# Eight-core retention block: the decay scales broadcast by TensorE instead of by DMA

## The chip, the cores and the metric

The kernel runs on the 8 NeuronCores of one Trainium2 chip. Each core computes one batch element of the input, with the same program and the same weights; no core waits for another. The metric is the device time of the slowest core, in microseconds (us).

## The reference

For each of 8 batch elements, x is 2048 x 1024. A half-weighted feed-forward layer (layer norm, block quantization of activations and weight to a 6-bit grid, product, bias), a retention layer, and the feed-forward layer again:

```python
x = x + 0.5 * ffn(layernorm(x), weight, bias)
x = x + attn(layernorm(x), Wq, Wk, Wv, W_G, W_O)
x = x + 0.5 * ffn(layernorm(x), weight, bias)

def attn(X, ...):                       # H = 8 heads, DH = 128
    q, k, v = X @ Wq, X @ Wk, X @ Wv    # split into heads
    scores = q @ k.T / sqrt(DH)
    decay[n, m] = gamma[h] ** (n - m) if n >= m else 0
    ret = (scores * decay) @ v          # then normalized per head
    return silu(X @ W_G) * ret @ W_O
```

The kernels split the decay: q of position n is multiplied by gamma^n / sqrt(128) and k of position m by gamma^-m. These are two tables of 8 x 2048 numbers, one row for each head.

## The kernel before

One arena in SBUF is laid out by hand, and the program is a straight list of stages, written once and emitted for each engine by `emit(Ctx(...))`: `c.op` issues an instruction on its engine, `c.inc` counts a semaphore up, `c.wait` makes one engine wait. Each engine works in the order of the text. Nearly all instructions carry the line number of the helper `Ctx.op` (L60), so the trace is read by tiles. In PSUM, `pbig` is 128 x 1024 float32, `psc` is 128 x 2048 float32 (four slots of 512), `pt0` and `pt1` hold transposes.

The stages are: FFN 1 with weight preparation (up to about 550 us); layer norm, transposes into `tt_sb` and the spill of x to HBM (to 620); then for each of wq, wk, wv, wg a `load_weight` and a projection (to about 941); the heads (to 1341); `load_weight("wo")` and the output projection (to 1424); FFN 2.

`load_weight` (lines 552 to 567) brings a 1024 x 1024 float32 weight in eight 512 KB tiles through two staging buffers and casts each to bf16 on VectorE. It begins when VectorE has done everything before it, and TensorE waits for its last cast.

`project_featmajor` (lines 569 to 614) is the stage that changes. It runs once for q and once for k. For each head `hc` there are four pieces `nb` of 512 positions. A piece is eight 128x128 by 128x512 bf16 matmuls into one of the four `psc` slots, and then one VectorE multiply of the slot by the head's scales, which writes the bf16 result. TensorE may be four pieces ahead of VectorE. The scales lie in `gam_sb`, four buffers of 128 x 2048 float32: `gam_dma` fills one with a DMA on SP's queue that reads one 8 KB row of the table 128 times (`partition_broadcast`), 1 MB for each head. Four such loads are issued as the projection begins, and the load for head `hc + 4` after head `hc` is done. ScalarE has no work in this stage.

`x_mm` (lines 430 to 451) in the FFN is not changed, but it holds the operation that the change brings: after eight full matmuls in each half it adds the bias with two matmuls of one row, `ones_row` (1 x 128) against `bias_hi` and `bias_lo` (1 x 512). So each of its calls issues 20 matmuls, of which 4 have one row.

Of the kernel before, what the change touches and what calls it, by code (L numbers as in the profile page):

```python
# [7 lines left out]
F32 = mybir.dt.float32  # L8
BF16 = mybir.dt.bfloat16
# [7 lines left out]
S = 2048  # L17
H = 8
# [65 lines left out]
def build_program(stop_after="full"):  # L84
    nc = bass.Bass("TRN2", target_bir_lowering=False)
# [2 lines left out]
    w_dr = {nm: nc.dram_tensor(nm, [D, D], F32, kind="ExternalInput").ap()  # L88
            for nm in ("wq", "wk", "wv", "wg", "wo", "wf")}
    bias_dr = nc.dram_tensor("bias", [1, D], F32, kind="ExternalInput").ap()  # L90
    qsc_dr = nc.dram_tensor("qsc", [H, S], F32, kind="ExternalInput").ap()
    ksc_dr = nc.dram_tensor("ksc", [H, S], F32, kind="ExternalInput").ap()
    m128_dr = nc.dram_tensor("m128", [128, 128], BF16, kind="ExternalInput").ap()
    id_dr = nc.dram_tensor("ident", [128, 128], BF16, kind="ExternalInput").ap()
    out_dr = nc.dram_tensor("out", [S, D], F32, kind="ExternalOutput").ap()
# [9 lines left out]
    O_G = 131072  # L105
# [8 lines left out]
    pbig = ctx_mem.enter_context(nc.psum_tensor("pbig", [128, 1024], F32))  # L114
# [6 lines left out]
    def vf32(off, n):  # L121
        return A[:, off:off + 4 * n].bitcast(F32)

    def vbf(off, n):
        return A[:, off:off + 2 * n].bitcast(BF16)

    def vi32(off, n):
# [3 lines left out]
    qt_sb = vbf(O_X, H * S).rearrange("p (h n) -> p h n", n=S)  # L131
    kt_sb = vbf(O_X + 32768, H * S).rearrange("p (h n) -> p h n", n=S)
# [8 lines left out]
    wst_sb = [vf32(O_W + 16384, D), vf32(O_W + 20480, D)]  # L141
    strip_sb = [vbf(O_S, 1024), vbf(O_S + 2048, 1024),
                vbf(O_S + 4096, 1024), vbf(O_S + 6144, 1024)]
    gam_sb = [vf32(O_G, S), vf32(O_G + 8192, S),
              vf32(O_G + 16384, S), vf32(O_G + 24576, S)]
    xrow_sb = [vf32(O_S, D), vf32(O_S + 4096, D)]
    t2row_sb = [vbf(O_S, D), vbf(O_S + 2048, D)]
    wdrow_sb = [vbf(O_S, D), vbf(O_S + 2048, D)]
# [33 lines left out]
    ones_row = vbf(O_C + 10944, 128)[0:1, :]  # L182
# [8 lines left out]
    def emit(c: Ctx):  # L191
# [4 lines left out]
             in_=bias_dr.partition_broadcast(128)).inc("wa", 16)  # L196
        c.op("sync", "dma_start", out=id_sb, in_=id_dr).inc("wb", 16)
        x_ld = []
        for i in range(4):
            c.op("sync", "dma_start", out=x_sb[:, 4 * i:4 * i + 4, :],  # L200
                 in_=x_in[:, 4 * i:4 * i + 4, :]).inc("ld", 16)
# [294 lines left out]
        if stop_after == "ffn1":  # L496
            for i in range(4):
                c.op("gpsimd", "dma_start", out=out_v[:, 4 * i:4 * i + 4, :],
                     in_=x_sb[:, 4 * i:4 * i + 4, :]).inc("g", 16)
# [18 lines left out]
        if stop_after == "ln2":  # L518
            c.fence()
            for i in range(4):  # L520
                c.op("gpsimd", "dma_start", out=out_v[:, 4 * i:4 * i + 4, :],
                     in_=x_sb[:, 4 * i:4 * i + 4, :]).inc("g", 16)
# [3 lines left out]
        for rc in range(RC):  # L526
# [10 lines left out]
            if stop_after != "t2nospill":  # L537
                c.wait("gpsimd", "v", vhere)
                c.op("gpsimd", "dma_start", out=xsp_dr[:, rc * D:(rc + 1) * D],
                     in_=x_sb[:, rc, :]).inc("g", 16)  # L540
        c.fence()
        if stop_after == "t2nospill":
            for i in range(4):
                c.op("gpsimd", "dma_start", out=out_v[:, 4 * i:4 * i + 4, :],
                     in_=x_sb[:, 4 * i:4 * i + 4, :]).inc("g", 16)
# [6 lines left out]
        def load_weight(nm):  # L552
            wcast_done = []
            c.wait("vector", "t")
            c.wait("sync", "v")
            for kc in range(KC):
                st = wst_sb[kc % 2]
                wsem = "wa" if kc % 2 == 0 else "wb"
                if kc >= 2:
                    c.wait("sync", "v", wcast_done[kc - 2])  # L560
                c.wait("sync", wsem)
                c.op("sync", "dma_start", out=st,
                     in_=w_dr[nm][kc * 128:(kc + 1) * 128, :]).inc(wsem, 16)
                c.wait("vector", wsem)
                c.op("vector", "tensor_copy", wbf_sb[:, kc, :], st).inc("v")
                wcast_done.append(c.cnt["v"])
            c.wait("tensor", "v")

        def project_featmajor(dst, sc_dr):
            piece = []  # L570
            gam_done = []
            gsems = ("wa", "wb", "wc", "wd")
            gam_ld = {}

            def gam_dma(h):
                gsem = gsems[h % 4]
                if h >= 4:
                    c.wait("sync", "v", gam_done[h - 4])
                c.wait("sync", gsem)
                c.op("sync", "dma_start", out=gam_sb[h % 4],  # L580
                     in_=sc_dr[h:h + 1, :].partition_broadcast(128)).inc(gsem, 16)
                gam_ld[h] = c.cnt[gsem]

            c.wait("sync", "v")
            c.wait("tensor", "v")
            c.wait("tensor", "s")
            for h in range(4):
                gam_dma(h)
            for hc in range(H):
                gsem = gsems[hc % 4]  # L590
                ld_here = gam_ld[hc]
                for nb in range(4):
                    i = len(piece)
                    half = psc[:, (i % 4) * 512:(i % 4) * 512 + 512]
                    if i >= 4:
                        c.wait("tensor", "v", piece[i - 4])
                    for kc in range(KC):
                        ins = c.op("tensor", "matmul", half,
                                   wbf_sb[:, kc, hc * 128:(hc + 1) * 128],
                                   tt_sb[:, kc, nb * 512:(nb + 1) * 512],  # L600
                                   start=(kc == 0), stop=(kc == KC - 1),
                                   skip_group_check=True)
                        if kc == KC - 1:
                            ins.inc("t")
                    c.wait("vector", "t")
                    c.wait("vector", gsem, ld_here)
                    c.op("vector", "tensor_tensor",
                         dst[:, hc, nb * 512:(nb + 1) * 512], half,
                         gam_sb[hc % 4][:, nb * 512:(nb + 1) * 512],
                         ALU.mult).inc("v")  # L610
                    piece.append(c.cnt["v"])
                gam_done.append(c.cnt["v"])
                if hc + 4 < H:
                    gam_dma(hc + 4)

        def project_rowmajor(dst3d, act):
            piece = []
# [24 lines left out]
                    piece.append(c.cnt["s"])  # L642

        load_weight("wq")
        project_featmajor(qt_sb, qsc_dr)
        load_weight("wk")
        project_featmajor(kt_sb, ksc_dr)
        load_weight("wv")
        project_rowmajor(v_sb, None)
        load_weight("wg")  # L650
# [8 lines left out]
        gn_rel_s = 0  # L659
        gn_rel_v = 0  # L660
        ret_done = {}
        for hc in range(_NHEADS):
            for nh in range(2):
                MMAX = 8 * nh + 8

                def emit_ret(mc, ev_v, ev_s, sbuf):
                    c.wait("tensor", "v",
                           max(ev_v, gn_rel_v if mc == 0 else 0))
                    c.wait("tensor", "s",
                           max(ev_s, gn_rel_s if mc == 0 else 0))  # L670
                    for ncc in range(max(mc, 8 * nh), 8 * nh + 8):
                        n8 = ncc - 8 * nh
                        ins = c.op("tensor", "matmul",
                                   pbig[:, n8 * 128:(n8 + 1) * 128],
                                   sbuf[:, n8 * 128:(n8 + 1) * 128],
                                   v_sb[:, mc, hc * 128:(hc + 1) * 128],
                                   start=(mc == 0 and n8 % 4 == 0),
                                   stop=(mc == ncc),
                                   skip_group_check=True)
                    ins.inc("t")  # L680
                    ret_done[(hc, nh, mc)] = c.cnt["t"]
# [3 lines left out]
                for mc in range(MMAX):  # L685
# [10 lines left out]
                    for nb in range(nblo, 2 * nh + 2):  # L696
                        slot = psc[:, (pp % 4) * 512:(pp % 4) * 512 + 512]
                        if piece_rel[pp % 4] is not None:
# [5 lines left out]
                             start=True, stop=True).inc("t")  # L704
                        there = max(c.cnt["t"], strip_guard)
                        nrel = nb * 512 - nh * 1024
                        if has_diag and nb == nblo:
# [6 lines left out]
                            if o + 128 < 512:  # L714
# [4 lines left out]
                                ev_s = c.cnt["s"]  # L719
# [4 lines left out]
                        else:  # L724
# [7 lines left out]
                            else:  # L732
# [3 lines left out]
                                ev_s = max(ev_s, c.cnt["s"])  # L736
# [5 lines left out]
                    if len(pending) > 2:  # L742
                        emit_ret(*pending.pop(0))
# [72 lines left out]
                gn_rel_s = c.cnt["s"]  # L816
# [6 lines left out]
        for rc in range(RC):  # L823
            rsem = "ga" if rc % 2 == 0 else "gb"
            if rc >= 2:
# [3 lines left out]
                 in_=xsp_dr[:, rc * D:(rc + 1) * D]).inc(rsem, 16)  # L829
# [4 lines left out]
            for jh in range(2):  # L834
                for kc in range(H):
                    ins = c.op("tensor", "matmul",
                               wp[:, jh * 512:(jh + 1) * 512],
                               zt_sb[:, kc, rc * 128:(rc + 1) * 128],
                               wbf_sb[:, kc, jh * 512:(jh + 1) * 512],
                               start=(kc == 0), stop=(kc == H - 1),  # L840
                               skip_group_check=True)
# [8 lines left out]
        if stop_after == "attn":  # L850
            for i in range(4):
                c.op("gpsimd", "dma_start", out=out_v[:, 4 * i:4 * i + 4, :],
                     in_=x_sb[:, 4 * i:4 * i + 4, :]).inc("g", 16)
# [6 lines left out]
    with nc.Block() as block:  # L860
        @block.sync
        def _(e):
            emit(Ctx(nc, "sync", sems))

        @block.vector
        def _(e):
            emit(Ctx(nc, "vector", sems))

        @block.scalar
        def _(e):  # L870
            emit(Ctx(nc, "scalar", sems))

        @block.tensor
        def _(e):
            emit(Ctx(nc, "tensor", sems))

        @block.gpsimd
        def _(e):
            emit(Ctx(nc, "gpsimd", sems))
# [6 lines left out]
def _host_consts():  # L886
    n = np.arange(S, dtype=np.float64)
    h = np.arange(H, dtype=np.float64)
    gam = 1.0 - np.exp2(-5.0 - h)
    qsc = ((gam[:, None] ** n[None, :]) / math.sqrt(DH)).astype(np.float32)  # L890
    ksc = (gam[:, None] ** (-n[None, :])).astype(np.float32)
    i = np.arange(128)
    m128 = (i[None, :] >= i[:, None]).astype(ml_dtypes.bfloat16)
    ident = np.eye(128, dtype=ml_dtypes.bfloat16)
    return qsc, ksc, m128, ident


# [20 lines left out]
```

How the kernel before makes its waits and increments, by code:

```python
    def inc(self, sem, n=1):  # L42
        self.ctx.cnt[sem] += n
        if self.inst is not None:
            self.inst.then_inc(self.ctx.sems[sem], n)
        return self
# [16 lines left out]
    def wait(self, eng, sem, val=None):  # L63
        v = self.cnt[sem] if val is None else val
        if v <= 0:
            return
        if self.cur == eng:
            getattr(self.nc, eng).wait_ge(self.sems[sem], v)
```

## Time and profile before

| | us |
|---|---|
| time before, median of 2 runs | 1815.59 (1814.21 to 1816.97) |
| the profiled execution | 1816.77 |
| its span on the slowest core (core 1) | 1815.2 |
| spans of the eight cores | 1809.5 to 1815.2 |
| TensorE busy | 837.3 (46%) |
| VectorE busy | 990.3 (55%) |
| ScalarE busy | 540.2 (30%) |
| DMA moved | 81.27 MB |

PE is TensorE's matmuls, PEld its weight loads, DVE is VectorE, ACT is ScalarE, SP issues DMAs. No engine is busy throughout: the stages have different limits, so the averages above don't tell what one stage is bound by. Times in the rows are microseconds from the start of the span. PEclk is the granted clock of TensorE as a share of 2.4 GHz: 1.00 is 2.4 GHz and 0.50 is 1.2 GHz.

### The profile page before, as it was taken

Reading aid. Unit: us, or ns where it says so; the run is one execution under the profiler, and the core shown is the slowest. Engines: PE = TensorE matmul, PEld = TensorE weight load, DVE = VectorE, ACT = ScalarE, POOL = GpSimd, SP = SyncE. Lnnn points to the kernel's source line nnn. Section 1 sums busy time; section 2 is a strip of 40 time slices with the busy share of each in tenths; the row PEclk is TensorE's granted clock in tenths of the full one; section 3 lists DMA queues with packets and bytes.
Section 4 is the critical chain, followed back from the end, with each engine's and each line's share of the span. In section 5 each row is a group of like instructions: output and inputs, shape, how many; then the busy total and the mean of one; then the engine's idle time right before and its main releaser. Section 6 shows DMA issues by size and latency. Waiting matters only on the chain.

```text
span 1815.2 us, 15305 instructions; the slowest of 8 cores (1809.5 to 1815.2 us)
## 1 busy us (share of the span) xinstructions
PE 837.3 (46%) x3904; PEld 358.4 (20%) x3904; DVE 990.3 (55%) x1289; ACT 540.2 (30%) x1414; POOL 29.7 (2%) x53
## 2 busy tenths in 40 slices
PE   0001144445432484949675445554429304544455
PEld 0000011111111132424233223332214101111111
DVE  2998878888831233320114454454433168888884
ACT  0445222222147400003234434444420542222220
POOL 0000000000000100000000000000001000000000
PEclk9999986666665587979896677766669756666666
DMA  7100100000002462530200000000034200000000
GB/s 233 35 23 1 47 0 0 0 1 0 0 0 81 170 214 93 186 116 1 70 1 1 1 1 1 1 1 1 1 108 124 93 0 24 24 23 35 23 24 35
DMA packets 19043, 81.27 MB, mean 45 GB/s; under 512 B 2192, under 2 KB 2192, under 8 KB 16656
## 3 DMA queue, kind: packets, MB, share of 16 engines
q1 hardware_dynamic: 11904, 53.02, 9.1%
q0 software_dynamic: 7056, 27.27, 4.1%
q8 instruction: 37, 0.61, 0.1%
q14 instruction: 46, 0.38, 0.1%
HBM read 61.41 MB, written 18.87 MB: 44 GB/s over the span
## 4 chain that ended last, share of the span: by engine, by line
PE 42%; DVE 25%; ACT 12%; issue 12%; DMA 6%; SPq 1%; DVEq 1%; ACTq 0%; POOL 0%; POOLq 0%
PE psc L60 34%; DVE arena L60 25%; ACT arena L60 12%; PE pt L60 4%; PE pbig L60 4%; DMA arena<-wf 1%; DMA arena<-wo 1%; DMA arena<-wq 1%; DMA arena<-wk 1%; DMA arena<-wv 1%; SPq L60 1%; DMA arena<-wg 1%; DVEq L68 1%; ACTq L68 0%; ACT L60 0%
## 5 line engine op out<-in xcount | busy, mean ns | idle before, releaser
L60 PE MATMUL psc<-arena 128*128 128x512 bf16 (+1 forms) x2240 | 652.1, 444 | 133.7 <-DVE arena L60 114.4
L60 PE MATMUL pt<-arena 128*128 128x128 bf16 x576 | 137.4, 263 | 832.0 <-ACT arena L60 598.8
L60 PEld LDWEIGHTS psc<-arena 128*128 128x128 bf16 (+1 forms) x2240 | 226.9, 107 | 484.7 <-issue 327.8
L60 DVE TENSOR_SCALAR arena<-arena 128x1024 f32<-128x1024 f32 (+4 forms) x348 | 169.2, 506 | 205.2 <-ACT arena L60 152.3
L60 DVE TENSOR_TENSOR arena<-arena 128x1024 f32<-128x1024 f32 (+2 forms) x220 | 249.5, 1134 | 24.3 <-DVE arena L60 1.8
L60 DVE SCALAR_TENSOR_TENSOR arena<-arena 128x1024 f32<-128x1024 f32 (+3 forms) x211 | 240.4, 1139 | 29.9 <-ACT arena L60 7.8
L60 PEld LDWEIGHTS pt<-arena 128*128 128x128 bf16 x576 | 60.0, 104 | 919.8 <-issue 907.6
L60 ACT ACTIVATE arena<-arena 128x1024 f32<-128x1024 f32 (+2 forms) x187 | 184.2, 986 | 144.3 <-DVE arena L60 135.3
L60 ACT CAST arena<-psc 128x512 bf16<-128x512 f32 (+1 forms) x224 | 106.2, 496 | 291.5 <-PE psc L60 250.6
L60 ACT CAST arena<-arena 128x1024 int32<-128x1024 f32 x40 | 41.8, 1045 | 505.4 <-DVE arena L60 505.4
L60 ACT COPY arena<-pt 128x128 bf16<-128x128 bf16 x576 | 138.8, 265 | 178.0 <-PE pt L60 175.0
L60 DVE TENSOR_TENSOR arena<-psc,arena 128x128 bf16<-128x128 f32 (+1 forms) x192 | 81.1, 424 | 195.6 <-PE psc L60 186.4
L60 DVE CAST arena<-arena 128x1024 bf16<-128x1024 f32 x42 | 29.1, 694 | 150.7 <-PE psc L60 57.8
L60 PE MATMUL pbig<-arena 128*128 128x128 bf16 x1088 | 98.4, 229 | 3.0 <-DVE arena L60 0.4
L60 DVE CAST arena<-psc 128x512 bf16<-128x512 f32 x96 | 66.3, 692 | 49.1 <-PE psc L60 47.0
L60 PEld LDWEIGHTS pbig<-arena 128*128 128x128 bf16 x1088 | 78.1, 103 | 42.5 <-issue 20.9
L60 DVE SCALAR_TENSOR_TENSOR arena<-psc,arena 128x1024 f32<-128x1024 f32 x32 | 39.2, 1225 | 67.3 <-PE psc L60 53.6
L60 DVE TENSOR_REDUCE arena<-arena 128x32 f32<-128x1024 f32 x40 | 48.5, 1213 | 30.2 <-DMA arena<-wf 27.5
L60 ACT ACTIVATE arena<-pbig 128x128 f32<-128x128 f32 x128 | 35.5, 277 | 44.2 <-DVE arena L60 33.9
L60 DVE TENSOR_TENSOR arena<-arena,psc 128x1024 f32<-128x1024 f32 x16 | 19.5, 1222 | 40.0 <-PE psc L60 40.0
L60 ACT ACTIVATE arena<-psc 128x512 bf16<-128x512 f32 x32 | 19.0, 597 | 33.9 <-PE psc L60 33.9
L60 DVE TENSOR_TENSOR arena<-pbig,arena 128x1024 f32<-128x1024 f32 x16 | 19.6, 1225 | 10.0 <-ACT arena L60 10.0
(14 smaller groups left out, 114.3 us busy)
## 6 DMA issues: line engine op xcount, KB each, us to landing
arena<-x SPq DMA_DIRECT2D x4, 2048.0 KB, 21.1
xspill<-arena POOLq DMA_DIRECT2D x16, 512.0 KB, 3.3
arena<-qsc SPq DMA_DIRECT2D x8, 1024.0 KB, 9.1
arena<-ksc SPq DMA_DIRECT2D x8, 1024.0 KB, 8.1
arena<-xspill POOLq DMA_DIRECT2D x16, 512.0 KB, 3.8
out<-arena POOLq DMA_DIRECT2D x16, 512.0 KB, 3.1
arena<-wf SPq DMA_DIRECT2D x8, 512.0 KB, 3.4
arena<-wq SPq DMA_DIRECT2D x8, 512.0 KB, 4.4
```

The source lines that it names most:

```text
L60: inst = getattr(getattr(self.nc, eng), name)(*a, **k)
L68: getattr(self.nc, eng).wait_ge(self.sems[sem], v)
```

## The change

The tables are handed over as pairs of bf16 rows, high and low part, and SP loads one high and one low row of 4 KB for each head into a single partition (`rows_dma`). TensorE broadcasts them: for each half of 1024 positions, four matmuls of `ones_row` against the rows write 128 x 1024 float32 scales to `pbig`, and ScalarE copies them to `gam_sb`. The second half uses the same `pbig`, so TensorE waits until ScalarE has copied the first. `gam_sb` has two buffers instead of four. The eight matmuls stand ahead of the head's 32. The rest of the program is unchanged, but for one wait of the heads stage that now also covers the last copy out of `pbig`.

```diff
-        def project_featmajor(dst, sc_dr):
+        pbig_sq = [0]
+
+        def project_featmajor(dst, hi_dr, lo_dr):
...
-            def gam_dma(h):
-                gsem = gsems[h % 4]
-                if h >= 4:
-                    c.wait("sync", "v", gam_done[h - 4])
-                c.wait("sync", gsem)
-                c.op("sync", "dma_start", out=gam_sb[h % 4],
-                     in_=sc_dr[h:h + 1, :].partition_broadcast(128)).inc(gsem, 16)
-                gam_ld[h] = c.cnt[gsem]
+            def rows_dma(h):
+                sh = "wa" if h % 2 == 0 else "wb"
+                sl = "wc" if h % 2 == 0 else "wd"
+                if h >= 2:
+                    c.wait("sync", "t", row_t[h - 2])
+                c.wait("sync", sh)
+                c.op("sync", "dma_start", out=hrow_sb[h % 2][0:1, :],
+                     in_=hi_dr[h:h + 1, :]).inc(sh, 16)
+                ld_h[h] = c.cnt[sh]
+                c.wait("sync", sl)
+                c.op("sync", "dma_start", out=lrow_sb[h % 2][0:1, :],
+                     in_=lo_dr[h:h + 1, :]).inc(sl, 16)
+                ld_l[h] = c.cnt[sl]
...
-            for h in range(4):
-                gam_dma(h)
+            rows_dma(0)
+            rows_dma(1)
             for hc in range(H):
-                gsem = gsems[hc % 4]
-                ld_here = gam_ld[hc]
+                c.wait("tensor", "wa" if hc % 2 == 0 else "wb", ld_h[hc])
+                c.wait("tensor", "wc" if hc % 2 == 0 else "wd", ld_l[hc])
+                shalf = []
+                for half in range(2):
+                    c.wait("tensor", "s", pbig_sq[0])
+                    for cc in range(2):
+                        cols = half * 1024 + cc * 512
+                        c.op("tensor", "matmul",
+                             pbig[:, cc * 512:cc * 512 + 512], ones_row,
+                             hrow_sb[hc % 2][0:1, cols:cols + 512],
+                             start=True, stop=False, skip_group_check=True)
+                        ins = c.op("tensor", "matmul",
+                                   pbig[:, cc * 512:cc * 512 + 512], ones_row,
+                                   lrow_sb[hc % 2][0:1, cols:cols + 512],
+                                   start=False, stop=True,
+                                   skip_group_check=True)
+                        ins.inc("t")
+                    c.wait("scalar", "t")
+                    if hc >= 2 and half == 0:
+                        c.wait("scalar", "v", gam_done[hc - 2])
+                    c.op("scalar", "copy",
+                         gam_sb[hc % 2][:, half * 1024:half * 1024 + 1024],
+                         pbig[:]).inc("s")
+                    pbig_sq[0] = c.cnt["s"]
+                    shalf.append(c.cnt["s"])
+                gam_sh[hc] = shalf
+                row_t[hc] = c.cnt["t"]
+                if hc + 2 < H:
+                    rows_dma(hc + 2)
                 for nb in range(4):
...
                     c.wait("vector", "t")
-                    c.wait("vector", gsem, ld_here)
+                    c.wait("vector", "s", shalf[nb // 2])
                     c.op("vector", "tensor_tensor",
                          dst[:, hc, nb * 512:(nb + 1) * 512], half,
-                         gam_sb[hc % 4][:, nb * 512:(nb + 1) * 512],
+                         gam_sb[hc % 2][:, nb * 512:(nb + 1) * 512],
                          ALU.mult).inc("v")
                     piece.append(c.cnt["v"])
                 gam_done.append(c.cnt["v"])
-                if hc + 4 < H:
-                    gam_dma(hc + 4)
```

## Rows read from the trace of the kernel before

**Rows 1.** The page's first line: the span of the slowest core.

```profile
span 1815.2 us, 15305 instructions; the slowest of 8 cores (1809.5 to 1815.2 us)
```

**Rows 2.** Windows by stage: engines' busy us (instructions), PEclk, DMA share, GB/s.

```profile
571.00:620.60 49.60, 31.69 (x128) 13.44 (x128) 11.94 (x15) 31.79 (x128) 8.50 (x16) 0.50 0.43 170
...
643.06:702.60 59.54, 58.34 (x256) 25.65 (x256) 21.95 (x32) 0.00 (x0) 0.00 (x0) 0.95 0.45 142
702.60:724.66 22.06, 0.00 (x0) 0.00 (x0) 5.55 (x8) 0.00 (x0) 0.00 (x0) 0.53 0.59 190
724.66:783.70 59.04, 56.97 (x256) 25.21 (x256) 21.86 (x32) 0.00 (x0) 0.00 (x0) 0.97 0.40 143
...
1340.90:1363.90 23.00, 0.00 (x0) 0.00 (x0) 5.36 (x8) 0.00 (x0) 1.07 (x2) 0.50 0.74 229
```

**Rows 3.** Timeline of the q projection: start, us, engine, operation, count, [idle before].

```profile
643.06 32.24 SPq L60 DMA_DIRECT2D arena<-qsc  x8
...
643.26 58.34 PE L60 MATMUL psc<-arena 128*128 128x512 bf16 x256 [23.34 <-DVE arena L60]
```

**Rows 4.** Timeline of the k projection.

```profile
724.89 8.46 PE L60 MATMUL psc<-arena 128*128 128x512 bf16 x32 [23.28 <-DVE arena L60]
...
733.38 2.48 DVE L60 TENSOR_TENSOR arena<-psc,arena 128x512 bf16<-128x512 f32 x4 [8.85 <-PE psc L60]
...
734.21 48.51 PE L60 MATMUL psc<-arena 128*128 128x512 bf16 x224 [0.87 <-DVE arena L60]
```

**Rows 5.** Groups of instructions by shape: count, busy us, mean ns of one.

```profile
L60 ACT CAST arena<-psc 128x512 bf16<-128x512 f32 x128 | 75.2, 587 | 248.9 <-PE psc L60 248.9
...
L60 PE MATMUL psc<-arena 1*128 1x512 bf16 x128 | 49.0, 470 | 0.0
...
L60 ACT CAST arena<-psc 128x128 bf16<-128x128 f32 x32 | 8.5, 266 | 10.9 <-DVE arena L60 8.9
```

**Rows 6.** TensorE weight loads in FFN 2, at the upper clock.

```profile
1506.25 1.41 PEld L60 LDWEIGHTS psc<-arena 128*128 128x128 bf16 x8 [0.62 <-issue]
1508.09 0.11 PEld L60 LDWEIGHTS psc<-arena 1*128 1x128 bf16 x2 [0.42 <-issue]
```

**Rows 7.** Instructions that write psc: duration ns minimum, median, maximum.

```profile
L60 PE MATMUL psc<-arena x2240: 374/379/634, 220.3 to 1805.6; 128*128 128x512 bf16 x177, 1*128 1x512 bf16 x10
```

**Rows 8.** Timeline of transposes in the heads stage: TensorE to ScalarE and back.

```profile
958.86 0.50 PE L60 MATMUL pt<-arena 128*128 128x128 bf16 x2 [12.71 <-DVE arena L60]
959.22 0.50 ACT L60 COPY arena<-pt 128x128 bf16<-128x128 bf16 x2 [4.73 <-PE pt L60]
...
959.63 0.54 PE L60 MATMUL pt<-arena 128*128 128x128 bf16 x2 [0.27 <-ACT arena L60]
```

**Rows 9.** DMA issues: count, KB each, median us from issue to landing.

```profile
out<-arena POOLq DMA_DIRECT2D x16, 512.0 KB, 3.1
...
arena<-ident SPq DMA_DIRECT2D x1, 32.0 KB, 3.8
```

**Rows 10.** SP's issues of q's scales: duration ns minimum, median, maximum.

```profile
L60 SPq DMA_DIRECT2D arena<-qsc x8: 327/328/1744, 643.1 to 675.0; - x8
```

**Rows 11.** Windows as the projections begin, columns as in the second group.

```profile
643.20:649.20 6.00, 5.94 (x15) 2.06 (x16) 0.00 (x0) 0.00 (x0) 0.00 (x0) 0.50 0.63 203
...
724.80:727.80 3.00, 2.91 (x8) 1.03 (x9) 0.00 (x0) 0.00 (x0) 0.00 (x0) 0.51 0.22 74
727.80:730.80 3.00, 3.00 (x15) 1.36 (x14) 0.00 (x0) 0.00 (x0) 0.00 (x0) 1.00 1.05 358
```

**Rows 12.** Timeline: one call of x_mm in FFN 1.

```profile
344.11 8.66 PE L60 MATMUL psc<-arena 128*128 128x512 bf16 x20 [0.61 <-ACT arena L60]
```

**Rows 13.** Windows in that call, and after the matmuls of a head.

```profile
344.10:352.10 8.00, 7.99 (x19) 2.16 (x19) 5.83 (x6) 0.71 (x1) 0.00 (x0) 0.50 0.00 0
...
976.30:980.30 4.00, 0.18 (x1) 0.03 (x1) 1.23 (x1) 1.93 (x11) 0.00 (x0) 1.00 0.00 0
980.30:984.80 4.50, 0.00 (x0) 0.00 (x0) 1.88 (x7) 1.22 (x7) 0.00 (x0) 0.50 0.01 2
```

More of the change, by code:

```diff
@@ L90, in build_program @@
     bias_dr = nc.dram_tensor("bias", [1, D], F32, kind="ExternalInput").ap()
-    qsc_dr = nc.dram_tensor("qsc", [H, S], F32, kind="ExternalInput").ap()
-    ksc_dr = nc.dram_tensor("ksc", [H, S], F32, kind="ExternalInput").ap()
+    qsch_dr = nc.dram_tensor("qsch", [H, S], BF16, kind="ExternalInput").ap()
+    qscl_dr = nc.dram_tensor("qscl", [H, S], BF16, kind="ExternalInput").ap()
+    ksch_dr = nc.dram_tensor("ksch", [H, S], BF16, kind="ExternalInput").ap()
+    kscl_dr = nc.dram_tensor("kscl", [H, S], BF16, kind="ExternalInput").ap()
     m128_dr = nc.dram_tensor("m128", [128, 128], BF16, kind="ExternalInput").ap()
@@ L143, in build_program @@
                 vbf(O_S + 4096, 1024), vbf(O_S + 6144, 1024)]
-    gam_sb = [vf32(O_G, S), vf32(O_G + 8192, S),
-              vf32(O_G + 16384, S), vf32(O_G + 24576, S)]
+    gam_sb = [vf32(O_G, S), vf32(O_G + 8192, S)]
+    hrow_sb = [vbf(O_G + 16384, S), vbf(O_G + 20480, S)]
+    lrow_sb = [vbf(O_G + 24576, S), vbf(O_G + 28672, S)]
     xrow_sb = [vf32(O_S, D), vf32(O_S + 4096, D)]
@@ L567, in load_weight @@
             c.wait("tensor", "v")
-        def project_featmajor(dst, sc_dr):
+        pbig_sq = [0]
+        def project_featmajor(dst, hi_dr, lo_dr):
             piece = []
             gam_done = []
-            gsems = ("wa", "wb", "wc", "wd")
-            gam_ld = {}
-            def gam_dma(h):
-                gsem = gsems[h % 4]
-                if h >= 4:
-                    c.wait("sync", "v", gam_done[h - 4])
-                c.wait("sync", gsem)
-                c.op("sync", "dma_start", out=gam_sb[h % 4],
-                     in_=sc_dr[h:h + 1, :].partition_broadcast(128)).inc(gsem, 16)
-                gam_ld[h] = c.cnt[gsem]
+            row_t = {}
+            ld_h = {}
+            ld_l = {}
+            gam_sh = {}
+            def rows_dma(h):
[11 more added lines that the diff above has]
+                ld_l[h] = c.cnt[sl]
             c.wait("sync", "v")
@@ L644, in emit @@
         load_weight("wq")
-        project_featmajor(qt_sb, qsc_dr)
+        project_featmajor(qt_sb, qsch_dr, qscl_dr)
         load_weight("wk")
-        project_featmajor(kt_sb, ksc_dr)
+        project_featmajor(kt_sb, ksch_dr, kscl_dr)
         load_weight("wv")
@@ L669, in emit_ret @@
                     c.wait("tensor", "s",
-                           max(ev_s, gn_rel_s if mc == 0 else 0))
+                           max(ev_s,
+                               max(gn_rel_s, pbig_sq[0]) if mc == 0 else 0))
                     for ncc in range(max(mc, 8 * nh), 8 * nh + 8):
@@ L891, in _host_consts, with split @@
     ksc = (gam[:, None] ** (-n[None, :])).astype(np.float32)
+    def split(t):
+        hi = t.astype(ml_dtypes.bfloat16)
+        lo = (t - hi.astype(np.float32)).astype(ml_dtypes.bfloat16)
+        return hi, lo
+    qsch, qscl = split(qsc)
+    ksch, kscl = split(ksc)
     i = np.arange(128)
@@ L894, in _host_consts @@
     ident = np.eye(128, dtype=ml_dtypes.bfloat16)
-    return qsc, ksc, m128, ident
+    return qsch, qscl, ksch, kscl, m128, ident
 def kernel(L0_attn_X, L0_attn_Wq, L0_attn_Wk, L0_attn_Wv, L0_attn_W_G,
@@ L906 @@
         np.asarray(L0_ffn_bias, dtype=np.float32).reshape(1, D))
-    qsc, ksc, m128, ident = _host_consts()
+    qsch, qscl, ksch, kscl, m128, ident = _host_consts()
     nc = build_program(_STOP_AFTER)
@@ L911 @@
     for b in range(8):
-        m = dict(x=X[b], bias=bias, qsc=qsc, ksc=ksc, m128=m128, ident=ident)
+        m = dict(x=X[b], bias=bias, qsch=qsch, qscl=qscl, ksch=ksch,
+                 kscl=kscl, m128=m128, ident=ident)
         m.update(ws)
```

## The prediction

> **What bounds the kernel now.** I read the spans of the page first [rows 1], then the windows by stage, because the change touches only the two projections of q and k. In their windows the reader is to see TensorE busy 58.34 of 59.54 us and 56.97 of 59.04 us, VectorE about 22, ScalarE 0, and a DMA share near 0.4 [rows 2]. Then the timelines: q's 256 matmuls run as one block, though eight 1 MB broadcasts are issued beside them [rows 3]. In k's there is one hole of 0.87 us, ahead of the 33rd matmul: VectorE's first multiply came only at 733.38, when the scales had landed, and TensorE had to wait for a psc slot [rows 4]. After it 224 matmuls take 48.51 us, 0.2166 us each, at the upper clock [rows 4]. So both stages are bound by TensorE, and the broadcasts cost 0.9 us of the whole execution. Whatever is added to TensorE's stream here, and whatever makes it wait, lengthens the stage; and since each weight load begins only when VectorE has finished the stage, it lengthens the kernel.
>
> **The change, part by part.**
>
> *The 16 MB of broadcasts go.* This gives back the hole: -0.9. The weight load behind a projection gains nothing: wk's takes 22.06 us after q's broadcasts, and wo's, with no broadcast anywhere near, 23.0 [rows 2].
>
> *Eight one-row matmuls per head.* Each streams 512 columns like the others. The one-row form exists in the FFN (mean 470 ns at mixed clocks [rows 5], and the same minimum and median as its neighbours in the table of psc's writers, 374 and 379 ns [rows 7]), so I charge 0.2166: 8 x 0.2166 = 1.73 us per head. The change of height costs more: between the first load of eight full weights at 1506.25 and the first one-row load at 1508.09 lie 1.84 us [rows 6], where eight full matmuls alone take 1.73. That is 0.11 per change, and a head has two: 0.2.
>
> *TensorE waits for ScalarE's first copy.* The second half overwrites pbig. From the last matmul of the first half: it lasts 379 ns [rows 7], of which 216 are already charged, so 0.16. To ScalarE's start it is 0.09: a transpose of 0.27 that starts at 958.86 is followed by the copy at 959.22 [rows 8]. The copy of 128x1024 float32 out of PSUM does not occur in the trace. 128 columns take 266 ns and 512 take 587 [rows 5], 0.836 ns per column, which extended gives 587 + 512 x 0.836 = 1015 ns. Bounds: the fixed part is already in these rows, so not under 0.9; and two copies of 512 would be 1.17. I take 1.02. From copy end back to TensorE 0.14: the first transpose copy ends at 959.49 (0.27 after 959.22) and TensorE restarts at 959.63 [rows 8]. The stall is 0.16 + 0.09 + 1.02 + 0.14 = 1.41 us per head. Nothing covers it: TensorE works in order, and the 32 matmuls of the head are queued behind the waiting one. While it waits, VectorE has at most the last piece of the previous head left. The second copy costs nothing: TensorE is then in the head's first two pieces, 3.46 us, and VectorE needs that half only at the third. Without this cover it would be another 1.4 per head. The two gam_sb buffers cost nothing either, since ScalarE refills one that VectorE left a whole head ago.
>
> Per head 1.73 + 0.2 + 1.41 = 3.34 us, and for 16 heads 53.5 us.
>
> *The row loads.* From the third head on, a row pair is issued as soon as TensorE has used the buffer, some 9 us before it is needed, with nothing else on SP's queue; the longest small landing in the page is 3.8 us [rows 9]. Hidden. The first pair is not: TensorE used to start at once when the weights were cast (643.26, SP's first issue being 643.06 [rows 3]) and now waits for the low row, issued second. A 4 KB transfer to one partition does not occur. The shortest landing is 3.1 us for 512 KB [rows 9]; at the 358 GB/s that a stretch of k's projection moves [rows 11] 1.5 us of it is moving bytes, which leaves 1.6. With one issue ahead of it, 0.33 [rows 10], and a hand-over of 0.1, TensorE starts 2.0 late, and at the most 4.2 (by 3.8). I take 2.3: twice 4.6.
>
> *The clock's rise.* q's matmuls ran at 0.50 for their first 5.9 us, k's for 2.9 [rows 11]. The late start and the first stall can make k's rise as late as q's: 3.0 us more at half speed, +1.5. Below it could be 0, or -1.5.
>
> Sum at an unchanged clock: 53.5 + 4.6 + 1.5 - 0.9 = 58.7 us.
>
> *The clock's fall.* This is the term that I am least sure of, and the largest unknown. In each head TensorE now runs 3.34 us without a single full-height matmul: eight one-row matmuls with a stall in the middle. Do one-row matmuls hold the clock up? The FFN says no. One call of x_mm runs 20 matmuls back to back from 344.11 [rows 12], four of them with one row, TensorE is busy 7.99 of 8.00 us, and the clock is still 0.50 at 352.1 [rows 13]; k's projection, all full height, was at 1.00 after 2.9 us and q's after 5.9 [rows 11]. The transposes tell the same of another kind of matmul: 31.69 us busy of 49.60 and 0.50 throughout [rows 2]. As for the fall: after a head's matmuls the clock stayed at 1.00 through 980.3 and was at 0.50 then, with 0.18 us of TensorE work in these 4.0 us [rows 13]. So a gap of about four us suffices, and one of 0.87 in k's projection did not bring it down (its window shows 0.97 over the stage, and the missing 0.03 is the start [rows 2, 4]). The new gap of 3.34 lies much nearer to the first. A fall costs half of the time until the clock is back: 2.9 to 5.9 us, so 1.5 to 3.0 us of loss. Over 16 heads that is 0 if none falls, and 16 x 3.0 = 48 if each does. Whether a given head falls should depend on how its gap happens to lie, and so differ between cores; the slowest of eight sets the time, so I take two thirds of the upper bound, +31.
>
> The Trainium skill (TensorE: Matmul & The Clock Gate, the table of "Why this matters for your kernels") warns of gaps between bursts in which the PE is idle. By its words the one-row matmuls would count as work, the idle gap would be only the stall of 1.41 us, the clock would hold, and the sum would stay at 58.7. The same page says under "Part 4: PE-mode transpose" that a transpose does not count as busy in the same way, and by that rule, the trace agrees; of one-row matmuls it says nothing.
>
> Total: 58.7 + 31 = 89.7 us. The profiled execution took 1816.8; the median of the runs is 1.2 lower. 1816.8 + 89.7 - 1.2 = 1905.3, rounded to 1905.
>
> **The rivals.**
>
> *The clock holds* (0.25). One-row matmuls count as work, or 3.34 us is too short. Against it stands the x_mm call; for it, that no gap between 0.87 and 4 us at the upper clock is shown with its outcome. 1816.8 + 58.7 - 1.2 = 1874.3, and 1868 to 1879 with the bounds of the starts and the copy.
>
> *Every head falls, or the hand-over is slower too* (0.08). 58.7 + 48 = 106.7 gives 1922; a copy of 1.17 us adds 16 x 0.15 = 2.4, so 1925, and more if the clock is also low during the one-row matmuls themselves.
>
> *Not slower* (0.03). The weight loads speed up, because eight cores no longer read the broadcast rows from the shared HBM. Casting eight tiles is 5.55 us of a 22.06 us load [rows 2], so a load could lose 16.5 at the very most. The four loads behind the first projection would give 66, against 58.7: 1816.8 + 58.7 - 66 - 1.2 = 1808. It decides only from 14.7 us per load on, and only if the clock holds. Against it: wo's load, without broadcasts, is the longer one, 23.0 [rows 2].
>
> *My forecast*, a fall in part of the heads (0.64), 1885 to 1922.
>
> **How the numbers follow.** The predicted time is that of the likeliest case, 1905. The range goes down into the case of the held clock, 1872, and up to every head falling, 1924; it leaves out about 2 in 10, half of the held clock among them. By about 2% can a measurement of this kernel be told from no change, which is 36 us: slower by more than that needs over 1852, and both large cases lie above it, even the one of the held clock by 22. Slower 0.97; within 2% 0.02, and faster 0.01, from the case of quick weight loads.
>
> **What would show each step.** In the profile after: per head a group of 8 one-row matmuls into pbig, a hole of about 1.4 us in TensorE ahead of the fifth, released by ScalarE, and ScalarE copies of 128x1024 of about 1.02 us, 32 of them. The windows of the two projections should be about 59.5 + 26.8 + 2.3 + the clock's share, so 88 us each if the clock holds and near 104 on the slowest core by my forecast. PEclk there is 0.95 and 0.97 now; if it stays over 0.93, the held clock is right, and if it drops under 0.85 in at least one projection, the fall is. The DMA queue of SP should show no wait of TensorE for a row load but the first of each projection. The prediction is wrong if ScalarE's copy takes over 1.2 us, if one-row matmuls stream slower than 0.22 us apart, or if later row loads arrive late.

## The result

| | before | after |
|---|---|---|
| median of all runs, us | 1816.99 | 1915.96 |
| lowest and highest | 1814.21 to 1853.13 | 1905.01 to 1945.18 |
| ratio to before | | 1.0541 (95% interval 1.0518 to 1.0565) |
| slowest core of the profiled run, us | 1815.2 | 1911.6 |
| fastest core of the profiled run, us | 1809.5 | 1876.6 |

The changed kernel is 5.4% slower; the forecast was 1905, with 1872 to 1924. A ratio is always taken within the same chip, and leaves disturbed runs out, the 1853 and the 1945 among them. One thing in the table is new beside the time: the cores, which lay within 5.7 us of each other, are now 35 us apart.

The spans and clocks of three cores of the changed kernel:

```profile
core 0: 1885.8 us, clock 0.736
core 1: 1876.6 us, clock 0.734
...
core 3: 1911.6 us, clock 0.719
```

The windows of the projections on core 3, which is the slowest, with the load of wk between them (columns as in [rows 2]):

```profile
640.10:745.44 105.34, 91.55 (x320) 33.38 (x320) 22.14 (x32) 16.19 (x16) 0.00 (x0) 0.79 0.00 1
745.44:767.30 21.86, 0.00 (x0) 0.00 (x0) 5.50 (x8) 0.00 (x0) 0.00 (x0) 0.58 0.61 192
767.48:880.54 113.06, 99.47 (x320) 35.25 (x320) 22.14 (x32) 16.20 (x16) 0.00 (x0) 0.73 0.00 1
```

They took 59.54 and 59.04 us in [rows 2] and take 105.34 and 113.06 here: +99.8 together, on the slowest core of either kernel. That is 3.4 more than the whole difference of the spans (96.4), because core 3 reached its q projection about 3 us earlier than the slowest core of before had (640.10 and 643.06). The weight load between them is the same (22.06 and 21.86). The granted clock fell from 0.95 and 0.97 to 0.79 and 0.73. The same windows on core 0:

```profile
641.66:742.09 100.43, 85.63 (x313) 32.38 (x320) 22.14 (x32) 16.19 (x16) 0.00 (x0) 0.83 0.00 1
763.24:852.50 89.26, 75.30 (x314) 29.93 (x320) 22.13 (x32) 16.19 (x16) 0.00 (x0) 0.94 0.01 1
```

For k, the same program with the same 320 matmuls takes 113.06 us on core 3 and 89.26 on core 0, and the clock is what differs, 0.73 and 0.94 (some matmul records are missing from core 0's rows). From SP's first row load of a projection to its first load of the next weight, all cores, in us:

| core | 0 | 1 | 2 | 3 | 4 | 5 | 6 | 7 |
|---|---|---|---|---|---|---|---|---|
| q | 100.4 | 95.7 | 100.5 | 105.3 | 100.5 | 113.5 | 95.5 | 103.8 |
| k | 89.3 | 89.2 | 89.1 | 113.1 | 89.0 | 89.0 | 113.4 | 89.3 |

k's values are two: 89, with the clock held from its first rise on, and 113. Read one head of each. First k on core 0 (this head is at the upper clock throughout; start, us, engine, what, count):

```profile
789.64 1.03 PE L60 MATMUL pbig<-arena 1*128 1x512 bf16 x4
...
790.82 1.01 ACT L60 COPY arena<-pbig 128x1024 f32<-128x1024 f32 x1 [7.02 <-PE pbig L60]
791.97 1.02 PE L60 MATMUL pbig<-arena 1*128 1x512 bf16 x4 [1.30 <-ACT arena L60]
...
799.94 1.03 PE L60 MATMUL pbig<-arena 1*128 1x512 bf16 x4
```

From head to head 10.30 us: four one-row matmuls, a hole that ScalarE's copy of 1.01 us ends, four more, and the 32. Now k on core 3:

```profile
797.71 1.03 PE L60 MATMUL pbig<-arena 1*128 1x512 bf16 x4
...
798.89 1.01 ACT L60 COPY arena<-pbig 128x1024 f32<-128x1024 f32 x1 [9.57 <-PE pbig L60]
800.04 1.77 PE L60 MATMUL pbig<-arena 1*128 1x512 bf16 x4 [1.30 <-ACT arena L60]
801.75 9.66 PE L60 MATMUL psc<-arena 128*128 128x512 bf16 x32
...
811.34 1.03 PE L60 MATMUL pbig<-arena 1*128 1x512 bf16 x4
```

The first four and the hole are the same. Then the second four take 1.77 instead of 1.02, the 32 take 9.66, and the head 13.63 us. Its windows:

```profile
797.70:800.00 2.30, 1.04 (x5) 0.29 (x4) 0.69 (x1) 1.01 (x1) 0.00 (x0) 1.00 0.00 0
800.10:806.80 6.70, 6.70 (x16) 2.12 (x17) 0.69 (x1) 1.01 (x1) 0.00 (x0) 0.51 0.00 1
806.90:811.30 4.40, 4.40 (x21) 1.85 (x19) 1.38 (x2) 0.00 (x0) 0.00 (x0) 0.99 0.00 0
```

The clock is 1.00 up to 800.0, goes to 0.50 as the second group of one-row matmuls begins, and is back after 6.7 us, in all of which TensorE was busy. Half of that time is lost: 3.3 us, which is 13.63 - 10.30.

Not each fall costs as much. In q on core 3 there are heads of this kind:

```profile
669.28 1.03 PE L60 MATMUL pbig<-arena 1*128 1x512 bf16 x4
...
671.61 1.02 PE L60 MATMUL pbig<-arena 1*128 1x512 bf16 x4 [1.30 <-ACT arena L60]
...
672.56 8.77 PE L60 MATMUL psc<-arena 128*128 128x512 bf16 x32
...
681.26 1.03 PE L60 MATMUL pbig<-arena 1*128 1x512 bf16 x4
```

This head takes 11.98 us, so 1.7 are lost, and the fall came only among the 32 full-height matmuls. The starts of the heads on all cores show three lengths from the second head on: 10.2 to 10.3 us (held), 11.9 to 12.0, and 13.6. They also show an order. In k, the heads 2 to 8 all held the clock on six cores and all lost it on cores 3 and 6. In q, cores 3 and 5 lost it in each of these heads. The other six held it for one to four heads, and from the first fall on they lost it in every head that was left. So on core 3 every head but the first of each projection had a fall, 14 in all: nine of 3.3 us and five of 1.7.

### The profile page after: what moved, and what is told of

The parts are those of the page before. It is cut to its first block, busy times and chain, and to the rows that moved or that the text cites. A ratio compares the mean times of both kernels' runs of the same rounds, so it can differ in the third digit from the quotient of the medians.

```text
span 1911.6 us, 15736 instructions; the slowest of 8 cores (1876.6 to 1911.6 us)
## 1 busy us (share of the span) xinstructions
PE 910.8 (48%) x4032; PEld 375.8 (20%) x4032; DVE 990.7 (52%) x1289; ACT 571.9 (30%) x1446; POOL 29.7 (2%) x53
## 4 chain that ended last, share of the span: by engine, by line
PE 44%; DVE 24%; ACT 13%; issue 11%; DMA 6%; SPq 1%; DVEq 1%; ACTq 0%; POOL 0%; POOLq 0%
PE psc L60 34%; DVE arena L60 24%; ACT arena L60 13%; PE pbig L60 6%; PE pt L60 4%; DMA arena<-wf 1%; DMA arena<-wq 1%; DMA arena<-wo 1%; DMA arena<-wk 1%; DMA arena<-wv 1%; SPq L60 1%; DMA arena<-wg 1%; DVEq L68 1%; ACTq L68 0%; ACT L60 0%
## 5 line engine op out<-in xcount | busy, mean ns | idle before, releaser
L60 PE MATMUL psc<-arena 128*128 128x512 bf16 (+1 forms) x2240 | 685.6, 461 | 84.3 <-DVE arena L60 65.2
L60 PEld LDWEIGHTS psc<-arena 128*128 128x128 bf16 (+1 forms) x2240 | 233.8, 111 | 466.7 <-issue 331.0
L60 DVE TENSOR_TENSOR arena<-arena 128x1024 f32<-128x1024 f32 (+2 forms) x220 | 249.5, 1134 | 24.3 <-DVE arena L60 1.8
L60 PE MATMUL pbig<-arena 128*128 128x128 bf16 (+1 forms) x1216 | 140.9, 253 | 74.5 <-DMA arena<-qscl 25.6
L60 PEld LDWEIGHTS pbig<-arena 128*128 128x128 bf16 (+1 forms) x1216 | 88.7, 102 | 138.9 <-issue 111.6
L60 ACT COPY arena<-pbig 128x1024 f32<-128x1024 f32 x32 | 32.4, 1012 | 221.2 <-PE pbig L60 221.2
L60 ACT ACTIVATE arena<-pbig 128x128 f32<-128x128 f32 x128 | 35.5, 277 | 44.8 <-DVE arena L60 33.9
L60 ACT ACTIVATE arena<-psc 128x512 bf16<-128x512 f32 x32 | 19.1, 597 | 33.9 <-PE psc L60 33.9
```

The source lines that it names most:

```text
L60: inst = getattr(getattr(self.nc, eng), name)(*a, **k)
```

## The experiments

Two theories stood against each other. A: one-row matmuls don't hold the clock, so what matters is how long TensorE goes without a full-height matmul. B: only idle time matters, here the stall of 1.4 us for ScalarE. The first four runs take the kernel before and put one suspect into it at a time (e2 is the control for e1). The added matmuls and copies of e1 to e4 and e7 compute nothing that is used, and these kernels are the kernel before otherwise.

### e1: 16 one-row matmuls and no wait

```diff
             for hc in range(H):
                 gsem = gsems[hc % 4]
                 ld_here = gam_ld[hc]
+                for e in range(16):
+                    c.op("tensor", "matmul",
+                         pbig[:, (e % 2) * 512:(e % 2) * 512 + 512],
+                         ones_row, bias_hi[0:1, 0:512],
+                         start=True, stop=True, skip_group_check=True)
```

> The kernel before (broadcasts by DMA) with 16 one-row matmuls ahead of each head's 32 and nothing that waits for them; their result in pbig is used by nobody. TensorE never idles. Their own cost is 16 heads x (16 x 0.2166 + 0.2) = 58.6 us. Theory A (one-row matmuls do not hold the clock): each head has 3.67 us without a full-height matmul, though TensorE is busy throughout, so the clock falls in many heads: 1895 to 1918 us, PEclk in the two projections under 0.8 on most cores. Rival B (only idle time lets the clock fall): PEclk stays at 0.9 or more and the time is about 1816 + 59 = 1875.

1911.35 us, ratio 1.0525 (1.0495 to 1.0556). The projections of its slowest core:

```profile
642.07:748.98 106.91, 105.72 (x384) 40.28 (x384) 22.13 (x32) 0.00 (x0) 0.00 (x0) 0.80 0.23 79
772.21:879.01 106.80, 105.42 (x384) 40.32 (x384) 22.13 (x32) 0.00 (x0) 0.00 (x0) 0.80 0.20 79
```

TensorE is busy 105.72 of 106.91 us, and the granted clock is 0.80. Rival B is out: an engine that never idles lost its clock. A had expected a clock under 0.8 on most cores, which did not come: in the 16 projections of the eight cores it was 0.80 to 0.83. The time is well inside A's range.

### e2: 16 full-height matmuls in their place

```diff
-                         ones_row, bias_hi[0:1, 0:512],
+                         wbf_sb[:, 0, 0:128], tt_sb[:, 0, 0:512],
```

> The same with 16 full-height matmuls (128 rows, real data) in place of the 16 one-row ones. Both theories expect the clock to stay: 16 x 16 x 0.2166 = 55.4 us, so about 1871. If the clock falls here too, it is not the height of the matmuls, and theory A is wrong.

1872.22 us, ratio 1.0310 (1.0280 to 1.0340). Slowest core:

```profile
641.04:728.16 87.12, 85.17 (x376) 38.19 (x384) 22.14 (x32) 0.00 (x0) 0.00 (x0) 0.97 0.30 97
749.88:835.52 85.64, 83.99 (x376) 37.81 (x384) 22.05 (x32) 0.00 (x0) 0.00 (x0) 0.98 0.28 99
```

The same number of columns, and 39 us less than e1. The clock stays at 0.97 and 0.98. Of the 39, 3 are the changes of height (16 x 0.2), the rest is the clock.

### e3 and e7: 8 and 12 one-row matmuls

The edit is that of e1 with 8 or 12 in place of 16.

> The same with 8 one-row matmuls per head, as many as the changed kernel has, but no wait for ScalarE. Cost 16 x (8 x 0.2166 + 0.2) = 30.9. Theory A: the stretch without a full-height matmul is 1.93 us, too short for a fall; 1848. If already 8 bring the clock down, it is over 1860, and the stall of the changed kernel was not needed for the loss.

1849.59 us, ratio 1.0185 (1.0156 to 1.0215), and PEclk 0.95 in both projections of the slowest core.

> The kernel before with 12 one-row matmuls ahead of each head, no wait: 2.8 us without a full-height matmul per head, TensorE never idle. Cost at an unchanged clock 16 x (12 x 0.2166 + 0.2) = 44.8, so 1861. Theory A expects falls in part of the heads, fewer than with 16: 1875 to 1892. At 1861 with PEclk over 0.9, a stretch of 2.8 us is too short.

1882.34 us, ratio 1.0367 (1.0344 to 1.0389). Slowest core:

```profile
640.45:737.55 97.10, 94.81 (x345) 36.92 (x352) 22.14 (x32) 0.00 (x0) 0.00 (x0) 0.81 0.26 87
759.35:848.31 88.96, 86.92 (x345) 34.97 (x352) 22.14 (x32) 0.00 (x0) 0.00 (x0) 0.88 0.26 95
```

In e3 each head after the first took 8.84 us, on every core; in e7 they took 9.7, about 11.4 or 13.0. So 1.93 us a head without a full-height matmul never let the clock fall, and 2.8 us did in part of the heads. Eight one-row matmuls alone, as many as the change brings, cost what the sum says (33.9 us against 30.9) and no clock. They needed the stall between them to become harmful.

### e4: the stall alone

```diff
             for h in range(4):
                 gam_dma(h)
+            # two full matmuls write pbig once
...
                 ld_here = gam_ld[hc]
+                c.wait("scalar", "t")
+                c.wait("scalar", "s")
+                c.op("scalar", "copy", sqscr, pbig[:]).inc("s")
+                c.wait("tensor", "s")
```

> The kernel before, with DMA broadcasts and no one-row matmul, but ahead of each head ScalarE copies pbig (128 x 1024, the result used by nobody) after TensorE's last matmul and TensorE waits for the copy. This is the stall of the changed kernel alone: 16 x 1.41 = 22.6 us, so 1839. Theory A: no fall, the idle stretch of 1.41 us is too short. Rival B: the idle time is what lets the clock fall, PEclk under 0.85 in the projections and 1860 or more.

1843.24 us, ratio 1.0150 (1.0121 to 1.0180), and PEclk 0.96 and 0.95. No fall, so the stall alone is harmless to the clock as well. Its price was a little higher than expected, 27.5 us instead of 22.6. The timeline shows why:

```profile
765.26 1.01 ACT L60 COPY arena<-pbig 128x1024 f32<-128x1024 f32 x1 [7.46 <-PE psc L60]
...
766.53 7.07 PE L60 MATMUL psc<-arena 128*128 128x512 bf16 x32 [1.41 <-ACT arena L60]
...
773.74 1.01 ACT L60 COPY arena<-pbig 128x1024 f32<-128x1024 f32 x1 [7.46 <-PE psc L60]
```

From copy to copy 8.48 us, of which the 32 matmuls are 6.93: 1.55 a head and not 1.41, so 24.8 for 16 heads. The remaining 2.7 us were not taken apart; the two matmuls that fill pbig once per projection and the later start of the first head are among them.

### e5: the second half moved behind two pieces

```diff
-                for half in range(2):
+                def scales(half):
                     c.wait("tensor", "s", pbig_sq[0])
...
+                scales(0)
                 for nb in range(4):
+                    if nb == 2:
+                        scales(1)
+                        if hc + 2 < H:
+                            rows_dma(hc + 2)
                     i = len(piece)
```

> The changed kernel with the second half's four one-row matmuls moved behind the head's first two pieces (16 full matmuls), so that ScalarE's copy of the first half is hidden and no stretch without full-height matmuls is over 1.07 us. By the sum of the prediction: 16 x (8 x 0.2166 + 4 x 0.1) = 34.1, starts 4.6, less 0.9 for the hole of the kernel before: 38 us without a fall, so 1855. Theory A: no fall, 1855. If the clock falls all the same, 1880 or more. A rival for the stall term (that the wait for ScalarE was already partly hidden) would give more than 1855 without a fall, since less than 16 x 1.41 = 22.6 would be saved.

1858.62 us, ratio 1.0235 (1.0216 to 1.0253). Against the changed kernel some 56 us are gained by the two ratios, by moving a few lines. Two projections of its slowest core:

```profile
641.10:720.13 79.03, 75.73 (x320) 29.11 (x320) 22.12 (x32) 16.19 (x16) 0.00 (x0) 0.94 0.01 2
741.68:819.75 78.07, 75.12 (x320) 28.96 (x320) 22.12 (x32) 16.19 (x16) 0.00 (x0) 0.95 0.01 1
```

78.07 instead of the 89.26 of a core of the changed kernel whose clock held in k: 11.2 a projection, which is 8 x 1.41 less two more changes of height per head, 8 x 0.2 (9.7), and 1.5 that the sum did not have. So nothing had hidden the stall. 0.94 and 0.95 say that the clock held.

### e6: the same broadcast, 128 rows high

```diff
+        c.op("vector", "memset", vbf(O_G + 16384, 4 * S), 0.0).inc("v")
+        c.op("vector", "memset", ones_full, 0.0).inc("v")
+        c.wait("vector", "v")
+        c.op("vector", "memset", ones_full[0:1, :], 1.0).inc("v")
...
-                             pbig[:, cc * 512:cc * 512 + 512], ones_row,
-                             hrow_sb[hc % 2][0:1, cols:cols + 512],
+                             pbig[:, cc * 512:cc * 512 + 512], ones_full,
+                             hrow_sb[hc % 2][:, cols:cols + 512],
```

> The changed kernel with the same eight broadcast matmuls and the same wait for ScalarE, but 128 rows high: the stationary operand has ones in row 0 and zeros in the others, and the moving rows 1 to 127 are zeros. Same number of columns, same stall, no change of height. Theory A by height: the clock holds, since the eight count as work and only 1.41 us is idle; 1816 + 16 x (1.73 + 1.41) + 4.6 + 1.5 - 0.9 = 1872. If it is the data that counts and not the height, rows of zeros hold the clock no better than one row: falls as in the changed kernel, 1895 to 1920. Rival B expects the falls of the changed kernel here too, since the idle time is the same.

1876.13 us, ratio 1.0328 (1.0310 to 1.0346), where this run's own sum gave 1872. This is the closest control: the order, the wait for ScalarE, the row loads and the number of matmuls are those of the changed kernel. Besides the height it changes one thing of known price, the two changes of height per head, 3 us in all. The added memsets take 7.3 us on VectorE near 527 us, in a stretch where it otherwise stands idle for 40.

```profile
640.83:727.64 86.81, 73.04 (x320) 31.25 (x320) 22.12 (x32) 16.19 (x16) 0.00 (x0) 0.95 0.01 2
750.16:837.10 86.94, 73.15 (x320) 31.20 (x320) 22.13 (x32) 16.19 (x16) 0.00 (x0) 0.95 0.00 1
```

```profile
777.33 1.02 PE L60 MATMUL pbig<-arena 128*128 128x512 bf16 x4 [1.30 <-ACT arena L60]
```

The hole of 1.30 us is still there, and the clock is 0.95. The eight cores are within 5 us of each other again (1869.2 to 1874.0). That 127 of the 128 rows held zeros made no difference: for the clock the height of the instruction counts here, not what is in the rows. By the two ratios some 39 us come back for three memsets, 3 of them from the changes of height and the rest from the clock.

### e9: both edits

> The two edits together: the second half's four broadcast matmuls behind the head's first two pieces, and all eight 128 rows high (ones in row 0, zeros elsewhere). Against the interleaved kernel with one-row matmuls it saves only the changes of height, 4 x 0.1 us per head, 6.4 in all; against the changed kernel it saves also the stall and the falls of the clock. 16 x 1.73 + 4.6 + 1.5 - 0.9 = 33: 1849. If changes of height cost nothing, it equals the interleaved one, 1858.

1849.24 us, ratio 1.0164 (1.0132 to 1.0196). It is the best form of the change that was found. It is 9.4 us under e5, which ran on another chip, where 6.4 were expected for the changes of height; within one program's trace a head takes 8.63 us here and 9.05 in e5, 6.7 for 16 heads. It is still 30 us slower than the kernel before: TensorE bounds the stage, and 128 more matmuls of 0.2166 us are 27.7 us that nothing can hide.

### e8 and e10: what the free space is good for

The rows of before show where these stages do lose time: TensorE stands for 23 us before the projections of q and k while eight tiles are loaded in pairs and cast [rows 2, 3, 4]. e8 issues the first two tiles of the next weight during the projection before it.

> The kernel before with the first two 512 KB tiles of wk, wv, wg and wo loaded during the projection before them, into staging buffers that are free then. The projections are bound by TensorE and SP has nothing to do in them, so each of the four weight loads should begin its casts at once instead of after a landing of 3.6 to 4.3 us: 4 x 4 = 16 us less, 1800. If the loads are paced by the casts' and transfers' chain so that the later tiles come no earlier, only the first landing of each is saved or nothing: 1801 to 1817.

1802.94 us, ratio 0.9931 (0.9915 to 0.9947): about 12.5 us less. It did not come evenly from the four loads. Averaged over the cores, TensorE's wait before v's projection fell from 23.2 to 18.7 us, before k's from 23.2 to 18.4, and before the output projection from 25.0 to 21.7; before wg's it stayed at 18.0. The kernel before already loads wg's first tiles ahead: its SP issues the first of them at 805.56, as v's projection starts, since VectorE has no work there that SP would have to wait for. The expected 16 us counted that load as well.

e10 does it in full. Two scale buffers in place of four, as in the change, but still filled by DMA; the 16 KB that this frees, and the rest of the region where it is unused, hold weight tiles:

```diff
-    gam_sb = [vf32(O_G, S), vf32(O_G + 8192, S),
-              vf32(O_G + 16384, S), vf32(O_G + 24576, S)]
+    gam_sb = [vf32(O_G, S), vf32(O_G + 8192, S)]
+    pre_sb = wst_sb + [vf32(O_G + 16384 + 4096 * i, D) for i in range(4)] + \
+        [vf32(O_G + 4096 * i, D) for i in range(2)]
...
+        def prefetch(nm, n):
+            c.wait("sync", "pa")
+            for kc in range(n):
+                c.op("sync", "dma_start", out=pre_sb[kc],
+                     in_=w_dr[nm][kc * 128:(kc + 1) * 128, :]).inc("pa", 16)
+            pre[nm] = (n, c.cnt["pa"])
...
+        prefetch("wq", 8)
...
+                if hc == 3:
+                    prefetch(nxt, 6)
```

> The kernel before, with two scale buffers instead of four (as the changed kernel has), still filled by DMA broadcast, and weight tiles loaded ahead: all eight of wq during the layer norm ahead of the projections, six of wk and wv during the projections into the freed 16 KB and the staging buffers, eight of wg during v's projection, two of wo. The casts, 8 x 0.83 us a weight, are then all that is left of wq's and wg's load (22 to 6.6), and for wk and wv the two last tiles land about 5 us after the casts begin, 22 to 8 or so. 15.4 + 14 + 14 + 15.4 + 4 = 63: 1754. If two scale buffers are too few (a 1 MB broadcast lands 8 to 14 us after its issue, a head takes 6.9), the projections of q and k wait for scales: up to 3 us a head lost, 16 x 3 = 48, and 1800.

1759.11 us, ratio 0.9670 (0.9630 to 0.9709): faster than both kernels. The timeline of its slowest core:

```profile
618.79 4.91 DVE L60 CAST arena<-arena 128x1024 bf16<-128x1024 f32 x8 [6.08 <-ACT arena L60]
...
624.09 51.45 PE L60 MATMUL psc<-arena 128*128 128x512 bf16 x224 [6.17 <-DVE arena L60]
...
677.41 2.48 DVE L60 TENSOR_TENSOR arena<-psc,arena 128x512 bf16<-128x512 f32 x4 [7.92 <-DMA arena<-qsc]
678.25 8.54 PE L60 MATMUL psc<-arena 128*128 128x512 bf16 x32 [2.72 <-DVE arena L60]
```

TensorE waits 6.17 us before q's projection instead of 23.34 [rows 3], since wq lies ready and its eight casts take 4.91 in a row. The smaller buffer showed up once: ahead of q's last head TensorE lost 2.72 us, because the scales' load was queued behind the six tiles of wk. By the ratio 60 us were saved, where 63 were expected, and wg's load, from 18.0 to 5.8, had less to give than the 15.4 that were put down for it.

## Why the prediction was right

The sign, the mechanism and the order of the size were right, and 1916 lies in the range. Point by point:

- **The broadcasts were hidden.** Right. With them gone the DMA share in the projections is 0.00, and no stage became shorter; the load of wk took 21.86 us against 22.06.
- **Eight one-row matmuls and two changes of height, 1.93 a head.** Right. e3 holds just these: 16 x 1.93 = 30.9 expected, 33.9 measured (1849.6 against 1815.7), and its heads take 8.84 us, 1.91 over the 6.93 of 32 matmuls.
- **The stall, 1.41.** Right in the changed kernel: the fifth one-row matmul starts 2.33 us after the first (797.71 and 800.04), of which 0.87 are four matmuls, so 1.46. The copy that no row of before showed took 1012 ns, against the 1015 extended from copies of 128 and 512 columns.
- **Per head 3.34.** With the clock held a head takes 10.30 us (core 0) less 6.93, so 3.37.
- **The start, 2.3 late.** Right. On core 3 SP issued its first row load at 640.10 and TensorE started at 642.57, 2.47 later, against 0.20 in [rows 3]; the difference is 2.27. The low row, issued at 640.81, let TensorE go after 1.76 us. Later row loads hid, as argued: between heads the trace shows no wait of TensorE for one.
- **A projection with the clock held:** 88 forecast, 89.0 to 89.3 measured on six cores.
- **The clock's fall: the cause right, the size not.** The fall was there, for the cause that was named, and PEclk fell below 0.85 as asked. The term was put at 31 us for the slowest core. It was 40: 105.3 + 113.1 less twice 89.2. On average over the cores it was 18.7. The step that was mis-sized is "two thirds of the upper bound", and both of its factors were off. Not two thirds of the heads fell on the slowest core but all of them after each projection's first. And the dearest fall cost 3.3 us and not 3.0, so 48 was no upper bound: the worst q projection lost 24.3 (113.5 less 89.2), more than half of it. It is partly luck that the term came within 9 us, because on core 3 the nine falls of 3.3 us were joined by five of only 1.7: 38 us together, and the rest lies in the first heads. In its mechanism the slowest core was nearer to the rival of every head falling, which had been given 0.08, while the other cores had falls in part of the heads.
- **The rule against it.** The Trainium skill (TensorE: Matmul & The Clock Gate, "Why this matters for your kernels") asks that TensorE should not idle for long between bursts. By this rule the changed kernel and e1 should have kept the clock. The runs disagree: e1's TensorE was busy 105.72 of 106.91 us at a clock of 0.80. The Trainium skill (same title, "Part 4: PE-mode transpose") says of transposes that they do not count as busy in the same way. Here that held of one-row matmuls too: 0.80 with 16 of them, 0.97 with 16 full ones.

The case that the clock holds had been put at 1874. e6, whose clock held, measured 1876; with the 3 us of the changes of height that it saves, the changed kernel would be at about 1879, so the sum without the clock is some 5 us low. The other 37 us up to 1916 are the clock, close to the 40 read on core 3. The total of 1905 is 11 low by these two.

Open is what decides, in a given execution, at which head a projection begins to lose the clock, and why it then goes on to the end. With one program the cores differ, and from run to run the time moves between 1905 and 1921, where the kernel before moves by some 4 us. That fits a dependence on how the heads' gaps lie against something that runs on its own, but this is not shown: no run set that relation and looked. Nor did a run let TensorE stand idle for more than about 1.5 us a head, so how an idle stretch of 3.3 us compares with one of one-row matmuls is not shown either.

## What to carry to other kernels

In a stage that TensorE bounds, as here, a transfer hidden beside it is nearly free (0.9 us), and replacing it by matmuls costs their whole length and each hand-over that they wait for; look at where the engine stands still, here ahead of each projection, and move the transfers there. When small matmuls are put into a dense stream, spread them among the full-height ones, or give them full height with zeros, since here eight of them together with a stall of 1.4 us halved the clock of part of the work that followed. Read the granted clock by stage and by core: eight cores that had run within 6 us of each other and were now 35 apart, with the same work, pointed to the clock.

## What the hardware showed

- One-row matmuls stream at the pace of full ones (four take 1.03 us), but they did not hold the clock as full ones do: 16 of them in a row per head brought 0.80 with TensorE busy 99% of the time, 16 full ones left 0.97 and 0.98.
- Full-height matmuls with zeros in 127 rows held the clock (0.95).
- Neither suspect alone did harm: 8 one-row matmuls 0.95, the stall 0.95 and 0.96; both together, 3.34 us a head, 0.73 to 0.94. In e7, 2.8 us of one-row matmuls gave 0.81 and 0.88.
- A fall in this kernel came in two sizes: heads of 13.6 us with 3.3 lost (6.7 us at 0.51, then 1.00 again), and heads of 11.9 to 12.0 us with 1.7 lost. Once a projection had begun to lose the clock, each of its later heads lost it too.
